# Attention loads issued in seven steps among the projected units, and the maxima over partitions taken by TensorE and VectorE

## What is computed

```
x = x + layernorm(attn(layernorm(x)))
x = x + layernorm(ffn(layernorm(x)))

attn:  q, k, v = split(h @ w_qkv.T + b_qkv)            # 16 heads of 32
       per head, in chunks of 128 tokens, with a state S that is carried on:
         inter  = (q * decay_q) @ S
         scores = (q @ k.T) * decaying causal mask
         S      = lam**128 * S + (k * decay_k).T @ v
       out = (inter + scores @ v) @ w_out.T + b_out
ffn:   gate, up = h @ fp8(gate_w) * s, h @ fp8(up_w) * s
       out = (silu(gate) * up) @ fp8(down_w) * s
```

## Time and profile before

| | |
|---|---|
| median of 3 runs | 1037.26 us (1037.1 to 1037.28) |
| the profiled execution, its own time | 1037.88 us |
| its span | 1036.1 us |
| TensorE matmul busy | 955.5 us, 92% |
| VectorE busy | 664.6 us, 64% |
| ScalarE busy | 526.3 us, 51% |
| GpSimd busy | 686.2 us, 66% |
| mean granted TensorE clock | 0.978 of full |
| SP's DMA queue | 157.86 MB, 68.7% of 16 engines' span |

### The profile page before, as it was taken

How to read it: one execution, slowest core, us unless ns; L and a number is a source line. 1 busy time by engine, 2 the same in 40 slices (tenths; PEclk the granted TensorE clock), 3 DMA queues, 4 the chain that set the end, 5 groups by cost and what they waited for, 6 DMA issues and landing times.

```text
span 1036.1 us, 21805 instructions
## 1 busy us (share of the span) xinstructions
PE 955.5 (92%) x8388; PEld 704.4 (68%) x8388; DVE 664.6 (64%) x1340; ACT 526.3 (51%) x997; POOL 686.2 (66%) x839
## 2 busy tenths in 40 slices
PE   1997988949988699999999999999999999999997
PEld 1775766636766486777867768677776787867774
DVE  7756767636478776666667656676666666666422
ACT  3535756535745563555635546355553555635432
POOL 2649898946765685676856768567585675856643
PEclk9998999979999899999999999999999999999999
DMA  9577989996899997494774947859477494732010
GB/s 342 142 208 196 253 203 254 214 266 180 192 194 225 204 195 143 113 184 89 147 146 110 183 88 149 152 104 184 91 145 140 115 184 94 144 69 42 26 37 21
DMA packets 297496, 159.79 MB, mean 154 GB/s; under 512 B 141616, under 2 KB 272688, under 8 KB 297264
## 3 DMA queue, kind: packets, MB, share of 16 engines
q1 hardware_dynamic: 296672, 157.86, 68.7%
q10 hardware_dynamic: 720, 0.54, 0.2%
HBM read 82.86 MB, written 41.94 MB: 120 GB/s over the span
## 4 chain that ended last, share of the span: by engine, by line
PE 48%; POOL 27%; DVE 8%; issue 8%; ACT 3%; SPq 2%; DMA 2%; POOLq 0%; DVEq 0%; ACTq 0%
PE bank L821 16%; PE bank L807 13%; PE att L784 8%; POOL att_pool L958 5%; POOL w_pool L972 4%; POOL hl L968 3%; POOL rstd L899 3%; PE bank L700 3%; PE bank L715 2%; POOL xr L964 2%; POOL rstd L903 2%; DVE stats L1206 2%; POOL vv L942 2%; DMA dram_qk<-qk_hl 2%; PE att L700 2%
## 5 line engine op out<-in xcount | busy, mean ns | idle before, releaser
L807 PE MATMUL bank<-f_pool,gate_q 128*128 128x256 f16 x1536 | 185.0, 274 | 5.4 <-DMA f_pool<-hl 4.4
L807 PE MATMUL bank<-f_pool,up_q 128*128 128x256 f16 x1536 | 183.4, 273 | 0.0
L821 PE MATMUL bank<-down_q,w_pool 128*128 128x512 f16 x768 | 168.3, 379 | 8.4 <-POOL w_pool L972 8.4
L958 POOL TENSOR_TENSOR att_pool<-p,att_pool 128x512 f16<-128x512 f32 x128 | 145.9, 1161 | 37.3 <-ACT att_pool L505 37.3
L807 PEld LDWEIGHTS bank<-f_pool,gate_q 128*128 128x128 f16 x1536 | 147.9, 98 | 26.3 <-DMA f_pool<-hl 4.6
L1337 DVE SCALAR_TENSOR_TENSOR w_pool<-bank,us_t,w_pool 128x256 f32<-128x256 f32 x192 | 84.0, 479 | 125.7 <-PE bank L807 100.1
L807 PEld LDWEIGHTS bank<-f_pool,up_q 128*128 128x128 f16 x1536 | 150.3, 98 | 17.5
L896 POOL TENSOR_TENSOR rstd<-mv,eps_t 128x1 f32<-128x1 f32 (+1 forms) x112 | 27.8, 249 | 192.4 <-DVE mv L1209 173.5
L821 PEld LDWEIGHTS bank<-down_q,w_pool 128*128 128x128 f16 x768 | 74.0, 98 | 96.7 <-issue 9.8
L972 POOL TENSOR_TENSOR w_pool<-w_pool 128x512 f16<-128x512 f32 x96 | 111.2, 1160 | 42.1 <-ACT w_pool L557 42.1
L505 ACT CAST att_pool<-p 128x512 f16<-128x512 f32 x128 | 76.7, 619 | 66.0 <-DVE p L1247 65.9
(11 more groups left out here) (139 smaller groups left out, 1800.1 us busy)
## 6 DMA issues: line engine op xcount, KB each, us to landing
xr<-in_x SPq DMA_DIRECT2D x32, 512.0 KB, 4.5
dram_qk<-qk_hl SPq DMA_DIRECT2D x64, 256.0 KB, 5.1
att_pool<-dram_qk SPq DMA_DIRECT2D x64, 256.0 KB, 6.8
f_pool<-dram_qk SPq DMA_DIRECT2D x64, 256.0 KB, 6.9
dram_v<-vv SPq DMA_DIRECT2D x32, 256.0 KB, 2.6
dram_kd<-kd_hl SPq DMA_DIRECT2D x32, 256.0 KB, 3.2
qn_pool<-dram_qk SPq DMA_DIRECT2D x32, 256.0 KB, 7.9
out_x<-w_pool SPq DMA_DIRECT2D x32, 256.0 KB, 2.1
```

Source lines behind the costliest of these rows:

```text
L807: ins = nc.tensor.matmul(b[:, j * TOK:(j + 1) * TOK], w[:, k, o * P:(o + 1) * P], x1_hl[:, v % 2, part, k], start=(k == 0 and part == 0), ...
L821: ins = nc.tensor.matmul((b_gate, b_up)[t][:, :], h_hl[:, part, k, t * P:(t + 1) * P], down_q[:, k], start=(k == 0 and part == 0), stop=(k ...
L958: nc.gpsimd.tensor_tensor(pr_hl[:, 1, heads(g)], by_head(p32[:, g % 2]), pr_hl[:, 0, heads(g)], ALU.subtract).then_inc(p_lo_d, 1)
```

## The change

Two things. The maxima over partitions are no longer taken by GpSimd: TensorE multiplies the column (one value per partition, broadcast over 128 columns, as the stationary operand) with a float32 identity matrix, which puts all 128 values on every partition, and VectorE reduces them from PSUM. The identity comes as a new constant input of 64 KB through ScalarE's queue, into the tile `state`, ahead of the five small loads there. One product serves w_qkv, ahead of k = 0; three serve w_out and the scales, ahead of k = 2. And `load_unit` of units 0 and 1 is cut in four steps each, issued by a table behind `ahead(6)` to `ahead(13)`, all but k = 10.

```diff
+        UNIT_STEPS = {6: ((0, 0),), 7: ((0, 1),), 8: ((0, 2),), 9: ((0, 3),),
+                      11: ((1, 0),), 12: ((1, 1), (1, 2)), 13: ((1, 3),)}
...
+            def load_unit(s, step=None):
+                if step in (None, 0):
+                    may_load(s)
+                    load_stack(s, 1, (0, 0, 1, 1))
+                if step in (None, 1):
+                    load_stack(s, 0, (0, 1, 0, 1))
+                if step in (None, 2):
+                    load_q(s)
+                    load_v(s)
+                if step in (None, 3):
+                    load_kt(s)
...
-                if k == LEAD - 6:
-                    load_unit(0)
-                if k == LEAD - 1:
-                    load_unit(1)
+                if k in UNIT_STEPS:
+                    for unit, step in UNIT_STEPS[k]:
+                        load_unit(unit, step)
...
+            act.dma_start(eye, eye_c).then_inc(eye_in, 16)
...
+            def spread(out, col):
+                return nc.tensor.matmul(out, small[:, col:col + 1].to_broadcast([P, P]), eye, start=True, stop=True)
+
+            def spread_w_max():
+                pe.wait_ge(eye_in, 16)
+                pe.wait_ge(w_max, 1)
+                spread(b_gate[:, 0:P], 5).then_inc(w_max_all, 1)
+
+            def spread_wout_max():
+                pe.wait_ge(wout_max, 1)
+                for n in range(3):
+                    ins = spread(b_up[:, n * P:(n + 1) * P], 20 + n)
+                ins.then_inc(wout_max_all, 1)
...
             def ahead(k):
+                if k == 2:
+                    spread_wout_max()
                 project_qk(k, 0)
...
-            pool.wait_ge(w_max, 1)
-            nc.gpsimd.partition_all_reduce(small[:, 6:7], small[:, 5:6], P, RMAX).then_inc(w_max_all, 1)
...
-                if k == 1:
-                    pool.wait_ge(wout_max, 1)
-                    nc.gpsimd.partition_all_reduce(small[:, 36:39], small[:, 20:23], P, RMAX
-                                                   ).then_inc(wout_max_all, 1)
...
                 dve.wait_ge(w_max_all, 1)
+                link(nc.vector.tensor_reduce(col(6), b_gate[:, 0:P], AX.X, ALU.max))
...
                 dve.wait_ge(wout_max_all, 1)
+                link(nc.vector.tensor_reduce(col(36, 3), b_up[:, 0:3 * P].rearrange("p (n q) -> p n q", n=3), AX.X,
+                                             ALU.max))
```

More of the change, by code:

```diff
@@ L13 @@
 AX = mybir.AxisListType
-RMAX = bass.bass_isa.ReduceOp.max
 P = 128
@@ L39, in sandwich @@
 def sandwich(nc, x, w_qkv_t, b_qk, b_v, w_out_t, b_out, gate_w, up_w, down_w, gate_s, up_s, down_s,
-             mask_c, decay_q_c, decay_k_c, lam_c, out):
+             mask_c, decay_q_c, decay_k_c, lam_c, eye_c, out):
     units = x.shape[0] // TOK
@@ L112, in sandwich @@
         state_hl = sb("state_hl", [P, 2, KT, P], F16)
+        eye = state[:, :, :].rearrange("p k d -> p (k d)")
         p32 = sb("p32", [P, 2, D])
@@ L133, in sandwich @@
         w_in = [sem(f"w_in{k}") for k in range(KT)]
+        eye_in = sem("eye_in")
         bias_in, tab_in, scl_in, wout_in, decay_in = (
@@ L331, in spill_v, with may_load @@
                     sp.dma_start(dram_v[n, t], vv[:, t]).then_inc(v_spilled[t], 16)
-            def load_unit(s):
+            def may_load(s):
                 if s >= 2:
@@ L341, in load_unit, with load_stack, load_q @@
                     sp.wait_ge(*((f_q_d, 12) if s else (w_lo_d, 6)))
[L342 to L348, removed]
+            def load_stack(s, which, parts):
+                sp.wait_ge(*((k_spilled if which else q_spilled), 32 * (s + 1)))
+                for r in range(4):
+                    sp.dma_start(stacks[s % 2][DH * r:DH * (r + 1), which],
+                                 dram_qk[s, which, parts[r]].rearrange("g (j d) t -> d (g j) t", d=DH)
+                                 ).then_inc(stack_in[s % 2], 16)
+            def load_q(s):
                 for part in range(2):
@@ L351, in load_unit, with load_v @@
                                  ).then_inc(q_in[s % 2], 16)
+            def load_v(s):
                 for t in range(T):
@@ L354, in load_unit, with load_kt @@
                 sp.dma_start(vva[s % 2], dram_v[s].rearrange("t p c -> p t c")).then_inc(v_in[s % 2], 16)
+            def load_kt(s):
                 sp.wait_ge(kd_spilled, 32 * (s + 1))
@@ L883, in slot @@
                 down(v, 1)
+            spread_w_max()
             for k in range(LEAD):
@@ L1482, in constants @@
         "lam_c": rows(lam ** P),
+        "eye_c": np.eye(P),
     }
```

## The result

| | before | after |
|---|---|---|
| median of the runs | 1037.27 us (1037.1 to 1037.91, 4 runs) | 1009.77 us (1009.25 to 1010.07, 4 runs) |
| span of the profiled execution | 1036.1 us | 1007.8 us |
| mean granted TensorE clock | 0.978 | 0.991 |
| last project_v of the projected units ends | 288.09 | 261.54 |

The ratio is 0.9733, with an interval of 0.9716 to 0.975: 27.5 us faster. The forecast was 1007.3 within 1002 to 1016.

The account below looks back on a forecast made before the run. Bound: a VectorE-GpSimd ring lengthened by idle time around the maxima, and SP held by unit 0's load. 5.3 + 9.8 + 17.4 - 1.5 - 1.0 = 30.0 us off 1037.88, median 0.6 lower: 1007.3 us, range 1002 to 1016.

Parts of the forecast that it names:

- First maximum: w_qkv's maximum, off GpSimd: scale 0.6 us sooner, v_sum(0) at 39.1 instead of 44.41, ring starts 5.3 us earlier.
- the ring: Loop of GpSimd's kd_lo and VectorE's k_lo, rounding, v_sum and moments in projected units; 16.70 us a round.
- Second maximum: Maxima of w_out and the scales: the ring's 26.48 us round becomes one of 16.70, saving 9.8 us.
- Load of unit 0: Stall in k = 10: next unit starts at 221.6, not 239.0, saving 17.4 us; steps cost 1.5, bounds 0 to 7.
- SP's free 4.8 us: SP's free time after the load of x, before kd's spill: first three steps fit, the last overruns by 2.2 us.
- such a wait is paid once: A wait from the load steps costs once, since TensorE then trails and the 16.70 us ring catches up.
- Given back: Last three projected units, tied to the ring again, take 50.1 us instead of 49.1: 1.0 us lost.
- Load of unit 1: Taking its 17.4 us of SP time out of early(0) gives 0, up to 2 us; nobody waited there.
- First rival: DMA engines become the bound: 1.9 us more in each of seven units, 13 instead of 1.5; 1019 us, chance 0.14.
- Second rival: Idle time behind the maxima on GpSimd is not theirs and stays: 1015.5 us, chance 0.05.
- Third rival: SP bound: every load step exposed on the ring, x of unit k+4 issued behind it; 1039.6 us, chance 0.02.
- Fourth: More than forecast: early(0) and early(1), with SP free 10 us sooner, save 3 to 5 us; 1003 us, chance 0.09.

Follow-up runs that it names:

- the maxima alone: Only the maxima part of the change, loads of units 0 and 1 whole behind k = 8 and k = 13, against the kernel before: 1023.49 us, ratio 0.9876.
- the changed kernel's second trace: The changed kernel run again with no edit, as yardstick for its set: 1010.37 us, ratio 0.9741 to the kernel before.

## Why the prediction came out right, and where its terms did not

- *First maximum, 5.3 us predicted, 3.56 measured.* The direction holds: without the idle times GpSimd no longer holds the ring back. But "v_sum(0) hangs on TensorE alone" is wrong. VectorE works without idle time from 20.36 up to v_sum(0) at 40.85, while TensorE's project_v(0) runs from 34.95 to 40.29, so v_sum's first half had its products by about the middle of that row; VectorE's own operations set the start. Two things in front of it were not priced. The scale comes no sooner at all (18.35 against 18.36, predicted 0.6): the identity's 64 KB stand ahead on ScalarE's queue, the first x lands at 4.96 instead of 4.23, and moving that DMA gives back up to 0.73. And L1166 and L1167 now fall beside GpSimd's x_lo and take 1.12 and 1.08 us instead of 0.15 and 0.16; moved away they give 39.34. Both moved, with the others, 38.36. I had let a new input go in for nothing.
- *Second maximum, 9.8 predicted, 9.82 measured.* The three products took 0.67 us from start to start and not 1.5, on TensorE where nobody waited.
- *Load of unit 0, 17.4 less 1.5 for the steps and less 1.0 given back.* Measured 13.17 against a net 14.9. The stall goes, as said. The steps cost more. By the prediction's own count the unit behind k = 10 would start, without steps and with the 13.38 measured for the maxima, at 221.6 - 13.38 = 208.2; it starts at 194.5 + 18.0 = 212.5, some 4.3 us later. Of these, 2.0 arise up to k = 8, whose successor starts at 178.24 (153.70 + 24.5) against 176.20 with the maxima alone, and k = 10 adds 1.7 (18.0 for 16.3). The remaining 0.6 are not the steps': the kernel with the maxima alone has them too, its sums of k = 9 start at 186.68 where 199.48 - 13.38 = 186.10 was due. So the steps cost 3.7 us and not 1.5.
- *Why the steps cost more.* Two steps of the prediction failed. It counted SP's free 4.8 us, but SP had room: the four steps held it for 2.14, 2.18, 1.6 and 2.58 us, and it began the spill of unit 7 at 157.15, as with the maxima alone. What the steps add is backlog on the DMA engines (share 1.13 in k = 8, 0.76 with the maxima alone), and the spill of unit 7 lands in 8.01 us behind them (the changed kernel's second trace) and in 5.98 where no step stands behind k = 6. And the prediction held that such a wait is paid once; it was paid in k = 8 and again in k = 10. So the cost fell behind the stack steps too, and not only where I had looked for it, at k = 9, 12 or 13. The 3.7 us are inside the bound of 7.
- *Given back, 1.0 predicted, 0 measured.* From k = 11 to 13 the units take TensorE's 16.3 us, 212.5 to 261.5: TensorE, late from k = 8 and 10, trails the ring. So 17.4 - 0.6 - 3.7 - 0 = 13.1, against 13.17 measured.
- *Load of unit 1, 0 predicted.* The span behind the projected units is 1.75 us shorter, within the bound of 2, and early(0) has as much work as before (23.43 us in 26). But the 1.75 cannot be put down to this load: the second trace of the changed kernel has 747.7 us there, only 0.4 less than before, and the maxima alone, with the load whole, have 747.6. In the first trace 1.4 us come in early(1), where two rows ran at the full clock (0.83 us each) that took 1.36 and 1.49 before; the second trace of the same kernel has them at 1.33 and 1.49, and the maxima alone at 0.83. What this load gives is between 0 and 2 us and is not shown.
- *First rival (the DMA engines bound).* Its mechanism is real, its size was not: it takes about 2 us up to k = 8 and 1.7 in k = 10, not 1.9 in each of seven units. Units 7 and 9 took 16.3 us at shares of 1.01 and 1.03, and 11 to 13 did too.
- *Second rival* fell with the runs that put the maxima back. *Third rival:* its mechanism showed in one kernel, with 1.04 us. *Fourth:* at most 1.75 us of the 3 to 5.

So two terms were too high by 1.7 each, and early(0) on gave 1.75 in the traced execution: the sum of 30.0 met 28.3 of the spans, and the medians differ by 27.5. The second maximum and the vanished stall were understood; that the total came within 2.5 us owes something to luck, since the 1.75 are no part of the argument and do not repeat.

## To carry to other kernels

A cheap instruction with idle time ended by "issue" on both sides costs what stands around it: read the rows before and behind it, and count the one that falls into a ring of two engines at full length. When one engine is taken off the path, look for the next one in the rows: here it was VectorE with its own operations, and not TensorE. When a block of transfers is spread, counting the issuing queue's free time is not enough; look at the DMA share of the stretches that receive the steps, and at which spill stands behind them. Removing the last wait of one engine moves the meeting point with the slower ring to the next shared product, so gains of such edits need not add.

## What the runs showed of the hardware

- PARTITION_ALL_REDUCE, 0.38 us of work, has 5.6 to 6.2 us of idle time ahead and 7.5 to 10.9 behind it, in each of its uses. The Trainium skill, "GPSIMD Engine Reference", section 2.1, has a load of about 6 us on the first call: the side ahead agrees (5.63 to 6.16 us, in each use that was traced); the side behind is not in it, and the runs show it.
- Two-input VectorE operations on a single column took 1.12 and 1.08 us beside GpSimd's x_lo, against 0.15 and 0.16 where GpSimd stood idle.
- Behind the wait in k = 8 the granted clock was at its lower level for a stretch. Behind 3.28, 4.07 and 5.83 us the three products of sum_squares already took 1.46 us; behind 4.29 they took 0.82, and only project_v behind them was slow, 7.03 us for 5.34. The two rows together lost 1.7 us behind waits of 3.28, 4.29 and 5.83, but 2.6 behind 4.07 and 2.8 behind 6.28 (the changed kernel's second trace), so the loss did not follow the wait's length.
- The transposing load holds SP for 6.98 us at the end of the block, and 2.58 us as a step of its own.
- The round from k = 4 to 5 took 18.73 us and not 16.7, since GpSimd's 1.5 us operation on one column takes 3.5 us there once. Only in this round does a VectorE operation of 2048 columns with two inputs stand beside it, and the two end within 0.15 us of each other. That looks like the operation above beside x_lo, but it was not tried.

```profile
113.02 3.53 POOL L943 TENSOR_SCALAR rstd<-mv,rstd 128x1 f32<-128x1 f32 x2
```

```profile
114.08 2.35 DVE L1212 SCALAR_TENSOR_TENSOR wout_hl<-qn_pool,small,wout_hl 128x2048 f16<-128x2048 f32 x1
```
